# Expert retrieval of the last 512 tokens moved from dense blocks to fetched table rows, under the next feed-forward stage

## The reference, cut to what matters

```python
# retrieval: 8 heads, 64 keys per half, 4096 experts, top 8 of 64 pairs per head -> 64 experts per token
s1, i1 = top_k(sim1, 8);  s2, i2 = top_k(sim2, 8)            # sims are linear in the normalised token xn
fs, pk = top_k(s1[..., :, None] + s2[..., None, :], 8)
fi     = (i1 * 64 + i2)[pk]                                   # expert numbers
hidden = gelu(xn . expert_down[fi]) * relu(fs)                # exact gelu
x      = x + sum_k hidden_k * expert_up[fi_k]
# low rank: a conditional base layer, then base + shared + 2 of 6 routed experts of rank 16 (softmax, top 2)
x      = x + L1_ffn(L1_cond(x))
# skills: two chosen skills and a shared one, width 1024 each, tanh gelu; its result y feeds the 4-bit layer
y      = sum over 3 of  w * (gelu(x @ gate) * (x @ up)) @ down
```

## Time and profile before

| | |
|---|---|
| median of 3 runs | 1827.57 us (1824.88 to 1829.73) |
| the profiled execution's own time | 1828.78 us |
| its span | 1827.1 us |
| begin | 0 to 117 us |
| peer | 117 to 802 us |
| lora | 802 to 858 us |
| skills | 858 to 1371 us |
| later stages | 1371 to 1827 us |

### The profile page before, as it was taken

One profiled execution on the slowest core, in us unless ns is written; L12 is line 12 of the kernel. 1 busy time (PEld: TensorE's weight loads), 2 busy tenths in 40 slices (PEclk: granted clock), 3 DMA queues, 4 the chain that ended last, 5 costly groups with the idle time before them and its releaser, 6 DMA issues. The chain is left out here.

```text
span 1827.1 us, 31945 instructions
## 1 busy us (share of the span) xinstructions
PE 1724.8 (94%) x13330; PEld 1074.9 (59%) x13330; DVE 915.5 (50%) x2460; ACT 370.8 (20%) x629; POOL 385.4 (21%) x271
## 2 busy tenths in 40 slices
PE   7988799999999999998999997999999997988998
PEld 3446678887888888874444443444444574448443
DVE  1359796867687777415111110111124796136676
ACT  2322112011111102001111111111113776133200
POOL 0003214132331415202988600000000000004000
PEclk9999899999999999999999998999999998998999
DMA  8000000000000001022312104000001261000000
GB/s 356 1 6 1 2 1 9 7 3 8 2 8 2 9 2 32 8 121 78 131 46 92 46 1 207 0 0 0 0 0 58 58 205 49 6 1 1 6 18 23
DMA packets 21659, 73.33 MB, mean 40 GB/s; under 512 B 3994, under 2 KB 8722, under 8 KB 18834
## 3 DMA queue, kind: packets, MB, share of 16 engines
q1 hardware_dynamic: 21522, 71.37, 10.8%
HBM read 69.26 MB, written 2.10 MB: 39 GB/s over the span
## 5 line engine op out<-in xcount | busy, mean ns | idle before, releaser
L614 POOL TENSOR_TENSOR peer_bm<-peer_bm,peer_slots 128x512 f32<-128x512 f32 x64 | 193.9, 3030 | 555.4 <-DVE peer_bm L701 555.4
L481 PE MATMUL peer_ps_h<-all_x,layer_down 128*128 128x256 f32 (+1 forms) x1024 | 241.7, 390 | 0.0
L481 PEld LDWEIGHTS peer_ps_h<-all_x,layer_down 128*128 128x128 f32 x1024 | 192.7, 193 | 28.5 <-issue 1.9
L520 PE MATMUL peer_ps_o<-peer_hg,layer_up 128*128 128x256 f32 x896 | 198.6, 380 | 0.4 <-DVE peer_hg L733 0.4
L1164 DVE SCALAR_TENSOR_TENSOR skills_hid<-skills_ps_u,all_pair_w,skills_act_g 128x512 f32<-128x512 f32 x64 | 48.1, 751 | 294.9 <-PE skills_ps_u L1126 294.9
L520 PEld LDWEIGHTS peer_ps_o<-peer_hg,layer_up 128*128 128x128 f32 x896 | 169.0, 190 | 28.6 <-issue 5.3
L496 PE MATMUL peer_ps_w<-peer_bm,peer_am 64*64 64x32 f32 x8192 | 139.2, 223 | 22.1 <-DVE peer_hg L733 14.4
L496 PEld LDWEIGHTS peer_ps_w<-peer_bm,peer_am 64*64 64x64 f32 x8192 | 131.4, 138 | 44.3 <-issue 44.2
L559 ACT ACTIVATE peer_hg<-peer_ps_h 128x512 f32<-128x512 f32 x128 | 76.5, 597 | 375.6 <-PE peer_ps_h L481 375.6
L1143 ACT ACTIVATE skills_act_g<-skills_ps_g 128x512 f32<-128x512 f32 x96 | 57.3, 597 | 438.3 <-PE skills_ps_g L1126 438.3
L703 DVE TENSOR_TENSOR peer_am<-all_iota_a,peer_slots 128x2048 f32<-128x2048 f32 x64 | 146.2, 2285 | 0.0
(11 more groups left out here) (311 smaller groups left out, 2299.4 us busy)
## 6 DMA issues: line engine op xcount, KB each, us to landing
quant_w<-in_l_w SPq DMA_DIRECT2D x38, 256.0 KB, 4.8
skills_ws<-in_l_w SPq DMA_DIRECT2D x8, 1024.0 KB, 4.8
all_early<-in_l_w SPq DMA_DIRECT2D x26, 256.0 KB, 3.9
four_skill<-in_skills SPq DMA_DIRECT2D x2, 3072.0 KB, 12.3
skills_w<-in_skills SPq DMA_DIRECT2D x2, 3072.0 KB, 15.1
skills_w<-in_skill_shared SPq DMA_DIRECT2D x2, 3072.0 KB, 22.2
layer_down<-in_down SPq DMA_DIRECT2D x1, 4096.0 KB, 25.2
layer_up<-in_up SPq DMA_DIRECT2D x1, 4096.0 KB, 35.7
```

The lines of the kernel that those rows point to most:

```text
L481: mm = pe.matmul(ps_h[group % 2][:, r, :], down[:, c, j * P:(j + 1) * P], g.x[:, c, bass.ds(i * PB, PB)], start=(c == 0), stop=(c == C - 1))
L520: mm = pe.matmul(ps_o[:, c, :], up[:, j, c * P:(c + 1) * P], hg[half][:, j, :], start=(j == 0), stop=(j == NJ - 1))
L614: pool.tensor_tensor(bm[c % RING][:], bm[c % RING][:], slots[half][:, 2, c * PAIRS:(c + 1) * PAIRS].unsqueeze(2).to_broadcast([P, PAIRS, WJ]),
```

## The change

The dense retrieval now covers tokens 0 to 1535 (6 blocks of 256; the loop in `peer` makes one pass instead of two). The last 512 tokens (block 3, four tiles of 128) are handled otherwise:

- `begin` builds a table `expert_rows` in HBM, 4096 rows of 2 KB: an expert's `down` row and its `up` row side by side. The up half is one HBM-to-HBM copy; the down half comes out of `g.down` by 8 DVE transposes of 128x1024 and 32 DMAs whose runs are 128 bytes long. SP waits for all of it before the stage ends.
- `peer` scores and picks tiles 0 and 1 of block 3 at its end and keeps their expert numbers and weights. The key map has a buffer of its own now; two rings share `g.early` and `g.route`, so the loads of the low-rank constants start after the last `weigh`.
- `lora` does three blocks. Its POOL queue issues the first 24 row fetches. The 4-bit peaks and scales leave it.
- `skills` goes block by block (96 steps, unrolled, 24 a block). Under steps 0 to 63, one chunk of 8 rows per token and 2 steps: POOL issues 8 indirect DMAs of 128 rows by 2 KB, DVE multiplies the down halves with xn (`product`), ACT sums each row by a copy with an accumulator and applies exact gelu (`hidden_rows`), DVE weighs and adds the up halves (`gather`, 8 dependent instructions). 32 chunks, a ring of three buffers. Tiles 2 and 3 are scored and picked in the first 20 steps. From step 65 to 72 block 3 gets its low-rank layer. From step 72 DVE does the 4-bit peaks and scales, the layer-3 mixing and `g.part` (`late`, a piece per step), and POOL only the rounding. The skill weights of batch 1 are loaded as soon as each is free (after steps 31 and 39), and the shared one once.

```diff
 begin, SP:
+            sp.dma_start(g.table[:, D:2 * D].rearrange("(j p) d -> p j d", p=P), a["up"]).then_inc(table_put, 16)
+            for i in range(C * 4):
+                sp.wait_ge(blocked_done, i + 1)
+                rows = g.table[i % 4 * part:(i % 4 + 1) * part, :].rearrange("(b i) d -> i b d", i=32)
+                for z in range(4):
+                    d0 = i // 4 * P + 32 * z
+                    sp.dma_start(rows[:, :, d0:d0 + 32],
+                                 blocked[i][32 * z:32 * z + 32, :].rearrange("i (b k) -> i b k", k=32)).then_inc(table_put, 16)
+            sp.wait_ge(table_put, 16 * (C * 4 * 4 + 1))
 begin, DVE, behind keep_fold(1):
+                if q == 1:
+                    dve.wait_ge(ahead, 32)
+                    for i in range(C * 4):
+                        dve.transpose(blocked[i], g.down[:, i // 4, i % 4 * part:(i % 4 + 1) * part]).then_inc(blocked_done, 1)
 peer:
-NPB = T // PB
+NPB = (T - BLK) // PB
+            late_scores(0)                                  # PE, behind the up product of the last block but one
+                    if c == 1 and j == 0:
+                        late_scores(1)                      # PE, in the middle of the last up product
+            for t in range(2):                              # DVE, before the last add_out
+                for _ in pick(NPB, t, late=True):
+                    pass
+def fetch_rows(pool, g, to, n):
+    per = SLOTS // RROWS
+    for k in range(RROWS):
+        at = n % per * RROWS + k
+        pool.indirect_dma_start(to[:, k, :], None, g.table, bass.IndirectOffsetOnAxis(ap=g.eid[:, n // per, at:at + 1], axis=0)
+                                ).then_inc(g.row_load[n % NRING], 16)
 skills, DVE:
+            def product(n):
+                dve.wait_ge(g.row_load[n % NRING], 16 * RROWS * (n // NRING + 1))
+                of = rows[n % NRING][:, :, 0:D]
+                dve.tensor_tensor(of, of, x.unsqueeze(1).to_broadcast([P, RROWS, D]), ALU.mult).then_inc(mul_done, 1)
+            def gather(n):
+                dve.wait_ge(act_done, (RROWS + 1) * (n + 1))
+                then(dve.tensor_tensor(wacts[:, n % 2, :], acts[:, n % 2, :], g.wgt[:, t, k0:k0 + RROWS], ALU.mult))
+                for k in range(RROWS):
+                        then(dve.scalar_tensor_tensor(out=to, in0=row, scalar=by, in1=to, op0=ALU.mult, op1=ALU.add))
+            for j in range(len(plan)):
+                hidden(j)
+                i = j // 2
+                if j % 2 == 0 and i + 1 < NCH:
+                    product(i + 1)
+                    next(picks, None)
+                if j % 2 == 1 and i < NCH:
+                    gather(i)
+                if j == TURN3:                              # 65
+                    outcome()
+                    chain = gates()
+                ...
+                if j > TURN3 + 6:
+                    next(rest, None)                        # late(): 4-bit peaks, scales, mixing, part
 skills, ACT:
+            def hidden_rows(n):
+                act.wait_ge(mul_done, n + 1)
+                for k in range(RROWS):
+                    row = rows[n % NRING][:, k, 0:D]
+                    act.activation(row, row, ACT.Copy, accum_out=dots[:, n % 2, k:k + 1]).then_inc(act_done, 1)
+                act.activation(acts[:, n % 2, :], dots[:, n % 2, :], ACT.Gelu).then_inc(act_done, 1)
 skills, POOL:
+            for n in range(NRING, NCH):
+                pool.wait_ge(vstep, marks["used", n - NRING])
+                fetch_rows(pool, g, rows[n % NRING], n)
+            pool.wait_ge(g.four.scaled, 6)
             g.four.rounded(pool)
-            (the mixing and the part, 30 and 120 instructions, now on DVE)
 skills, SP:
+            for s in range(2):
+                sp.wait_ge(d_ready, n_q + (s + 1) * M2)
+                load_skill(1, s)
+            sp.wait_ge(vstep, marks["used", NCH - 1])
+            sp.dma_start(g.held[:], a["q_w"]).then_inc(late_load, 16)
 lora:
-            g.four.scales(dve)
-                if q == 1:
-                    base(3)
```

More of the change, by code:

```diff
@@ L6 @@
+import itertools
 from contextlib import ExitStack
@@ L624, in _, with pick @@
         def _(dve):
-            def pick(i, t):
+            def pick(i, t, late=False):
                 n = i * PT + t
@@ L810, in _ @@
             pool.wait_ge(presets, 3)
+            for n in range(NRING):
+                fetch_rows(pool, g, (g.qw, g.held, g.ring2)[n][:, 0:RROWS * 2 * D].rearrange("p (k n) -> p k n", k=RROWS), n)
         @block.tensor
@@ L882, in _ @@
             logits(1)
-            low(3)
             logits(2)
-            logits(3)
-            for q in range(3):
+            for q in range(n_blk):
                 base(q)
@@ L890, in _ @@
             spread(0)
-            for q in range(NBLK):
+            for q in range(n_blk):
                 pe.wait_ge(hw_done, q + 1)
-                if q + 1 < NBLK:
+                if q + 1 < n_blk:
                     spread(q + 1)
@@ new lines, in skills @@
+        oneh = sums.rearrange("p h a b -> p (h a) b")
+        ij = s8[:].rearrange("p (z g) k -> p z (g k)", z=2)
+        cand = sums.rearrange("p h a b -> p h (a b)")
+        dots = sb("dots", [P, 2, RROWS])
+        acts = sb("acts", [P, 2, RROWS])
+        wacts = sb("wacts", [P, 2, RROWS])
+        at3 = slice(GAT * BLK, (GAT + 1) * BLK)
+        rows = [t[:, 0:RROWS * 2 * D].rearrange("p (k n) -> p k n", k=RROWS) for t in (g.qw, g.held, g.ring2)]
+        xt3 = [t[:, RROWS * 2 * D:RROWS * 2 * D + 2 * D] for t in (g.qw, g.held)]
@@ new lines, in skills @@
+        block3_step = sem("block3_step")
+        after = {}
+        for name, times in (("xt_ready", 1), ("xt_kept", C), ("t_ready", 1), ("t_done", C), ("h_ready", 1), ("hs_done", 1),
+                            ("l_ready", 1), ("ex_done", 1), ("wide_done", 1), ("w_ready", 1), ("hw_done", 1), ("o_ready", C), ("x_done", C)):
+            after[name] = sum(n for _, n in after.values()) + times, times
+        after = {name: n for name, (n, _) in after.items()}
+        block = st.block()
+        plan = [(q, s, m) for q in range(NBLK) for s in range(3) for m in range(M2)]
@@ new lines, in keep @@
+            def keep(q):
+                act.wait_ge(d_ready, (q + 1) * n_q)
+                if q == GAT - 1:
+                    act.wait_ge(block3_step, after["x_done"])
+                for c in range(C):
+                    act.activation(g.y[:, c, q * BLK:(q + 1) * BLK], acc[q % 2][c][:], ACT.Copy).then_inc(y_done, 1)
+            act.wait_ge(block3_step, after["xt_ready"])
+            for i in range(2):
+                act.activation(xt3[i], spare[i][:], ACT.Copy).then_inc(block3_step, 1)
@@ new lines, in _ @@
+            for j in range(len(plan)):
+                gelu(j)
+                if j == 0:
+                    hidden_rows(0)
+                if j % 2 == 1 and (j + 1) // 2 < NCH:
+                    hidden_rows((j + 1) // 2)
+                if j == TURN3 + 1:
+                    act.wait_ge(block3_step, after["h_ready"])
+                    act.activation(hs3, spare[0][0:LOW, :], ACT.Identity, bias=g.off[0:LOW, C:C + 1]).then_inc(block3_step, 1)
+                if j == TURN3 + 2:
+                    act.wait_ge(vstep, marks["l3_shift"])
+                    act.activation(ex3[:], logit3[:], ACT.Exp).then_inc(block3_step, 1)
+                if j > n_q and j % n_q == 1:
+                    keep(j // n_q - 1)
```

565 lines of the change are left out of this document (399 added, 166 removed).

## The result

The changed kernel takes 1772.58 us (median of 4, 1767.22 to 1776.86) against 1827.03 (1824.88 to 1829.73): ratio 0.9691, 95% interval 0.9667 to 0.9714, 55 us less. The forecast was 1722. The profiled execution has a span of 1767.5 us. So the direction was right and the time lies inside the stated range, but it is 8 us above the likeliest case's own range (1690 to 1765), and half of the gain that this case had promised is missing.

What follows compares the result with a forecast made beforehand. PE was taken as the bound, 1724.8 of 1827.1 us busy. Terms -164.4 + 6.8 + 8 - 11.3 - 12.3 + 19.4 + 4 - 1.2 + 33 + 12 gave -106, so 1722 us, range 1662 to 1830.

Steps and rivals of the forecast that it cites:

- likeliest case: Whole kernel: the forecast itself, all parts summed to 1722 us, own range 1690 to 1765, chance 0.44.
- Parts 1 and 2: peer: one loop pass less, -164.4, late scores on PE, +6.8; begin: building the expert table, +8.
- Part 3: lora: a block less, and peaks and scales gone from DVE, so the stage ends sooner, -11.3 (8 to 14).
- Parts 4 and 5: Batch gap: PE's skill-load wait goes, -12.3; skills: added PE work +19.4, waits for DVE +4, tail -1.2.
- Part 6: skills: ACT and DVE work per chunk, table loads at 1.28 us included, fits under PE's steps, 0.
- Part 7: skills from step 75: POOL's rounding locks out DVE's two-SBUF-operand mixing, delaying `hid` and PE, +33 (0 to 45).
- Rival A: Everything hidden: POOL's rounding holds up no DVE instruction and the table is ready at 117; 1669 us, chance 0.2.
- Part 8: skills: fetches at 1.3 us each on POOL make a chunk 10.65 us instead of 10.24, 29 chunks, +12.
- B: skills: fetches and DVE exclude each other for whole instructions, 13.7 us a chunk, +101 instead of 12; 1811, chance 0.13.
- C: skills: slow fetches stop PE each chunk; from 1.79 us a fetch slower than before, 1877 at 2.0; chance 0.11.
- D: begin: the expert table is late, +64 instead of +8; 1778 us, chance 0.12.

Runs made afterwards that it cites:

- e8: The changed kernel again, nothing altered, in a set without late ACT: 1750.17 us, ratio 0.957 to the kernel before.
- e9: The changed kernel with the 4-bit rounding moved from POOL to DVE, same set as e8: 1713.01 us, ratio 0.9364 to the kernel before.
- e4: The changed kernel with four of eight fetches per chunk left out in skills, part of the result missing: 1697.67 us, ratio 0.9273 to the kernel before.
- e10: The changed kernel with rounding on DVE and the product cut into eight instructions: 1689.49 us, ratio 0.9228 to the kernel before.
- e3: The changed kernel with the 128x2048 product on DVE cut into eight of 128x256: 1727.87 us, ratio 0.9433 to the kernel before.
- e1: The changed kernel with the 4-bit rounding on DVE instead of POOL, in four parts: 1713.72 us, ratio 0.9349 to the kernel before.
- e12: The kernel of e10 without batch 1's two skill loads, part of the result missing, late ACT: 1752.42 us, ratio 0.9572 to the kernel before.

## Why the prediction was right, and where it wasn't

The forecast is held first against e8, where ACT is not late (span 1744.5), then against the first record (1767.5).

- **Parts 1 and 2, peer and the table: -149.6 forecast, -163 to -164 measured** (lora begins at 639.8 in e8 and 638.2 in the first record, at 802.4 before). `add_out` comes six times, as read. Two terms were mis-sized. The table costs 0, its bound from below, not +8. SP's issue was 0.87 us a DMA (27.8 us for 32), not 1.5 to 2: the step from the earlier trace rows, length per run of a DMA, failed, as 1024 runs were issued in 1.3 to 1.7 times the 0.57 us of 256 runs. The step from the earlier trace rows failed too: the 2048 runs of an engine took 29 us (56 to 85), 14 ns each and not 36.5. The other 5 to 6 us are the two blocks. From the first `add_out` to the last but two are 411.1 us before and 241.1 after, so 170.0 went and not 164.4: the two blocks of the earlier trace rows, 356 to 524, took 84 us each, with 3.6 us of stops of PE in the second, while the other three took 80.5 to 81.7. The average over five took too little for what went. The late scores cost what was forecast: the last up product takes 35.9 us instead of 28.8, +7.1 (forecast +6.8).
- **Part 3, lora: -11.3 forecast, -12.7 in e8** (639.8 to 682.6), but **+7** in the first record. The mechanism was right. What it lacked is the late ACT, 20 us in this stage, which no row of the kernel before could show. "The 24 fetches issued here have 44 us, 1.8 each" was right: they took 30.
- **Parts 4 and 5: +9.9 forecast.** Not measured by themselves. Skills grew from 513 to 605.0 in e8; less 35.4 for the rounding (605.0 - 569.6 in e9) and 49.2 for the fetches (e4), 7.4 are left. No wait of PE for a skill load stands in the trace, as forecast.
- **Part 6: 0 forecast, 0 measured** (e4). A table load is 1.28 us in all of them, with the next activation right behind it (one load runs from 708.62 to 709.90, the next activation starts at 709.91), and ACT in e4 does its full work in PE's shadow. The Trainium skill, "ScalarE: Activation LUTs", on table sets, has about 2.7 us for a switch, which would have made it a loss; the measured switch decides against it.
- **Part 7: +33 forecast, 37.2 measured** between e8 and e9. The place and the two late `hid` came as worked out, 40.1 and 51.4 us behind the start of the rounding (forecast 41.5 and 53); the order did but for one mixing instruction more that got through at 1182.78. PE's two holes are 27.6 + 4.0 = 31.7 us, which is the forecast; by the rows of PE its half clock behind them adds 4 to 5, and the sum had no term for that. Rival A, that one-operand instructions on POOL hold nothing, is refuted by the row at 1167.92. The rule of the Trainium skill in "SBUF — State Buffer", on the two sides, is that the pair is locked for a whole instruction. The trace agrees but for the last 1.5 us of POOL's two long ones: DVE's held instructions end 0.76 before POOL's, and need 0.75 themselves (spans on POOL are rough).
- **Part 8: +12 forecast, +49 measured.** This is the step that failed, and by the prediction's own sign: "steps longer than 5.5 us before step 64" was to mean wrong, and a chunk of two steps takes 12.0 us in e8 and 12.1 in the first record, 6.0 a step. The 1.3 us a fetch looks right beside the 1.25 measured, but by luck: it was 1.04 for the fetch and 0.25 for DVE's exclusion, and an unheld fetch is 0.95 and 0.30 of pause before the next, with nothing of exclusion in it. Wrong was that "0.25", "mostly pieces of 0.48". The pieces do cost only 0.1 to 0.25 each, but the one product of 2.29 us falls on a fetch in 27 of the 32 chunks and adds 0.9 to 2.1 there (cutting it gained 23.5 us in all). The earlier trace rows had shown just that: a short instruction held for a whole L703 of this same size. And 10.4 us a chunk against 10.24 left no room for the ring: POOL waits for the weighing of three chunks ago (1.86 in the row of e8 above; 52 us in e10 in all, of which 17.8 before the first fetch of the stage), and a stop behind a skill load is not made up. Of the 26 us that e10 still has over e4, both without or less the rounding (546.0 and 555.8 - 35.4), some 8 to 11 stand beside the skill loads in DVE's waits; the rest wasn't separated.

Sum of the misses against e8, by stages: -13 (Parts 1 and 2), -1.4 (lora), -2.5 (Parts 4 and 5), +2.4 (Part 7 by stages, 35.4 against 33), +37 (Part 8), later stages +1: +23.5, and the forecast span of 1721 + 23.5 = 1744.5 is the profiled span of e8 (its median is 1750.17). So the verdict rests on a wide range and on misses that cancel in part: Part 8 alone was 37 us off. The remaining 22 us to 1772 are the late ACT: 20 in lora and 3 to 7 in skills (608.3 and 611.8 against 605.0).

Of the rivals, B (whole-instruction exclusion of fetch and DVE, 13.7 us a chunk) names the right mechanism too broadly: a fetch is held to the end of the DVE instruction it starts under, but it doesn't hold DVE, so the times don't add up. The chunk of 12.0 us lies about half way between the forecast's 10.65 and B's 13.7. C and D did not happen.

## What to carry to other kernels

Where DVE has an instruction with two operands in SBUF and POOL issues an indirect DMA or computes under it, count one hold for each meeting, to the end of the one that was there first: here 0.9 to 2.1 us for a fetch under a product of 2.29, and some 14 for a mixing instruction under one of POOL's of 15.8. Cut the long ones into short ones, or give both jobs to one engine; each was tried here on one case (e3, e1). A stage under which a second engine has work for nearly its whole time can be bound by that engine, as skills was here up to step 64; sum its holds and the ring's round trip before calling it hidden. Where the bound engine will stop, add its clock: here two holes of 31.7 us cost PE 4 to 5 more. And run a changed kernel in more than one set, with the old one beside it, before splitting a difference of 1% into causes.

## What the runs showed that was not expected

- In three of five sets ACT started late, by up to 10.6 us in the changed kernel and 15.5 in e12, with no releaser in the profile, and only in the stages and steps in which rows are fetched. The changed kernel itself ran in three sets and was late in two; there it costs 22 us or 1.2% of the whole. Whether instructions or semaphores come late to ACT is open, and so is whether the fetches cause it: no run in a late set was without them.
- An indirect DMA of 128 rows of 2 KB costs POOL 0.95 us and 0.30 to the next; SP issues a DMA of 1024 runs in 0.75 to 0.97 us.
- A long POOL instruction with one operand (15.8 us) holds DVE as one with two does, and a DVE instruction with one operand in SBUF was held too (L1295, 4.38 instead of 0.48). `hid`, with one operand in PSUM, ran in 0.74 under POOL's fourth instruction (1199.77).
- DVE did the rounding in 17 us that POOL did in 47.5.
